# A LoRA linear layer with a retrieval feed-forward in float32 on one core: the running sums in VectorE's order, one weight combination stored where it is made, and statistics once per batch

## The reference

```
h   = x @ W.T + base_bias + (x @ A[id].T) @ B[id].T        # [8, 512, 2048]
q   = h @ Wq.T;  scores = router(q);  top 8 of 512; softmax; weighted sum of aux_values
aux = (...) @ Wvd.T @ Wvu.T
var = variance of h over the 2048 features, per token
norm_var = log1p(var) / (mean over all 4096 tokens of log1p(var) + 1e-6)
learned  = gelu(h @ Wu1.T + bu1) @ Wu2.T + bu2
u    = clip(0.5 * norm_var + 2.5 * sigmoid(learned), 0, 5)
gate = sigmoid(gate_w1 * clip((u - 0.5) / 1.5, 0, 1) + gate_bias), 0 where under 0.05
out  = x + h + gate * aux
```

## Time and profile before

| | before |
|---|---|
| median of 3 runs | 1995.03 us (1994.07 to 2000.32) |
| the profiled execution's own time | 1995.2 us |
| its span on the core | 1993.4 us |
| mean granted TensorE clock | 0.989 |
| HBM read, written | 316.32 MB, 96.47 MB |

### The profile page before, as it was taken

The page is one execution under the profiler, slowest core; times in us unless marked ns, Lnnn a source line. Parts: engine busy times, 40 slices in busy tenths (PEclk is TensorE's granted clock), DMA queues, the critical chain, the costliest instruction groups (busy, mean ns, idle before and its releaser), DMA issues.

```text
span 1993.4 us, 24866 instructions
## 1 busy us (share of the span) xinstructions
PE 1943.9 (98%) x8682; PEld 1582.2 (79%) x8682; DVE 1262.0 (63%) x1656; ACT 693.7 (35%) x1051; POOL 400.9 (20%) x283
## 2 busy tenths in 40 slices
PE   8999999999999999999999999999999999999996
PEld 6877877888888888888888877777888888888875
DVE  5775688555467836546873643677377677667666
ACT  3422433333233433324333322344233323332332
POOL 2210122120022202002210100110433323233323
PEclk9989999999999999999999999999999999999997
DMA  7656777552367745146764434757977677777774
GB/s 268 229 190 244 254 252 258 168 173 74 131 202 232 225 147 187 45 154 210 234 208 140 159 106 171 240 184 236 326 269 270 231 244 236 229 241 237 274 275 164
DMA packets 195201, 414.46 MB, mean 208 GB/s; under 512 B 26692, under 2 KB 27716, under 8 KB 194950
## 3 DMA queue, kind: packets, MB, share of 16 engines
q1 hardware_dynamic: 150150, 324.78, 50.3%
q10 hardware_dynamic: 44928, 88.10, 11.5%
HBM read 316.32 MB, written 96.47 MB: 207 GB/s over the span
## 4 chain that ended last, share of the span: by engine, by line
PE 86%; DVE 7%; issue 3%; ACT 2%; DMA 2%; ACTq 0%; SPq 0%; DVEq 0%; POOL 0%; POOLq 0%
PE bank L1659 17%; PE bank L1660 17%; PE bank L1661 17%; PE bank L1697 6%; PE bank L1698 6%; PE bank L1699 6%; PE bank L1712 1%; PE bank L1713 1%; PE bank L1599 1%; PE bank L1600 1%; PE bank L1786 1%; PE bank L1788 1%; PE bank L1787 1%; DVE sums L1261 1%; PE bank L1767 1%
## 5 line engine op out<-in xcount | busy, mean ns | idle before, releaser
L1659 PE MATMUL bank<-xop,wsp 128*128 128x512 f32 x1792 | 710.7, 397 | 14.9 <-DVE wsp L1152 8.0
L1660 PE MATMUL bank<-xop,wsp 128*128 128x512 f32 x1792 | 701.8, 392 | 0.0
L1661 PE MATMUL bank<-xop,wsp 128*128 128x512 f32 x1792 | 700.9, 391 | 0.0
L1659 PEld LDWEIGHTS bank<-xop,wsp 128*128 128x128 f32 x1792 | 338.5, 189 | 98.6 <-DVE xop L1152 8.0
L1660 PEld LDWEIGHTS bank<-xop,wsp 128*128 128x128 f32 x1792 | 338.9, 189 | 74.5 <-issue 3.8
L1661 PEld LDWEIGHTS bank<-xop,wsp 128*128 128x128 f32 x1792 | 338.2, 189 | 72.4
L1152 DVE TENSOR_TENSOR wsp<-wraw,wsp 128x1024 fp32r<-128x1024 f32 x184 | 241.2, 1311 | 122.0 <-ACT wsp L790 121.7
L790 ACT ACTIVATE wsp<-wraw 128x1024 fp32r<-128x1024 f32 x184 | 194.0, 1054 | 204.3 <-PE bank L1661 170.9
L779 POOL TENSOR_TENSOR r_h<-r_h,r_x 128x512 f32<-128x512 f32 x128 | 172.7, 1349 | 363.7 <-DMA r_h<-h_dram 363.7
L877 ACT ACTIVATE stage<-stage 128x512 f32<-128x512 f32 x128 | 80.9, 632 | 406.1 <-DVE stage L1247 405.7
L1261 DVE TENSOR_TENSOR sums<-sums,stage 128x1024 f32<-128x1024 f32 x116 | 154.5, 1332 | 92.2 <-ACT stage L877 92.2
(11 more groups left out here) (158 smaller groups left out, 1957.9 us busy)
## 6 DMA issues: line engine op xcount, KB each, us to landing
wraw<-in_w SPq DMA_DIRECT2D x131, 512.0 KB, 3.8
xraw<-in_x SPq DMA_DIRECT2D x248, 256.0 KB, 4.2
wraw<-t_dram SPq DMA_DIRECT2D x80, 512.0 KB, 3.6
h_dram<-stage ACTq DMA_DIRECT2D x128, 256.0 KB, 3.9
hraw<-h_dram SPq DMA_DIRECT2D x128, 256.0 KB, 4.0
r_x<-in_x SPq DMA_DIRECT2D x128, 256.0 KB, 4.4
r_h<-h_dram SPq DMA_DIRECT2D x128, 256.0 KB, 3.5
out<-o_st ACTq DMA_DIRECT2D x96, 256.0 KB, 3.8
```

The lines of the kernel that those rows point to most:

```text
L1659: pe.matmul(ps, wsp[:, slot, 0, f], x_hi(i), start=(k == 0), stop=False)
L1660: pe.matmul(ps, wsp[:, slot, 0, f], x_lo(i), start=False, stop=False)
L1661: last = pe.matmul(ps, wsp[:, slot, 1, f], x_hi(i), start=False, stop=(k == HT - 1))
```

## The change

It has four parts. (1) `add_sums(g-2)` moves from the front of VectorE's step to its end, ahead of `finish(g-1)`. (2) T1 is stored by ScalarE's queue from `t_res` when `make_t1` has made it (`store_t1`), and `make_t2` waits for that store; M5 of pair 0 then loads T1 from `t_dram` as the other pairs do, two steps ahead, with nothing made or stored there. (3) `T4_AT` begins at step 16 and no longer at 18. (4) The statistics are gathered in one segment for each batch: M2 and M3 share a running sum, M4 and M5 the other. The passes stand in M3 and the next M1 at o = 3, and the one in M6 is gone. The last one moves to step 5 of row 0, with the steps that use it (variances 4 to 7, log 6 to 9, its sum 7 to 10, the mean's matmul 8 to 13, the mean 9 to 14).

```diff
-        T4_AT = {18 + o: o for o in range(HT)}
+        T4_AT = {16 + o: o for o in range(HT)}
         T3_AT = {M7 * HT - 3 + o: o for o in range(HT)}
-        T1B_AT = {M5 * HT - 3 + o: o for o in range(HT)}
...
-            early = p == 0 and q in (M7, M5)
+            early = p == 0 and q == M7
...
-            return kind == "t4" or kind == "tile" and g < PAIR and tile_of(g)[1] in (M7, M5)
+            return kind == "t4" or kind == "tile" and g < PAIR and tile_of(g)[1] == M7
...
-        SEGMENT = {M2: 0, M4: 1, M5: 1, M3: 2}
-        STATS_AT = {(M6, 1): 0, (M3, 2): 1, (M1, 2): 2}
+        STATS_AT = {(M3, 3): 0, (M1, 3): -1}
+
+        def segment(p, q):
+            return 2 * p + (q in (M2, M3))
+
+        def segment_of_batch(b):
+            return b ^ 1
+
+        def stats_at(p, q, o):
+            seg = 2 * p + STATS_AT[q, o] if (q, o) in STATS_AT else -1
+            return seg if seg >= 0 else None
...
                     else:
-                        if p == 0:
+                        if q == M5:
+                            sp.wait_ge(t_moved[o], 32)
+                        elif p == 0:
                             wait_stored(sp, "t4", o)
...
-                if p == 0 and q in (M7, M5):
-                    act.dma_start(t_dram[T3 if q == M7 else T1, o], src).then_inc(t_out[W_PLACE["tile", g] % NWR], 16)
+                if p == 0 and q == M7:
+                    act.dma_start(t_dram[T3, o], src).then_inc(t_out[W_PLACE["tile", g] % NWR], 16)
+
+            def store_t1(o):
+                act.wait_ge(t_ready, t_count("t1", o))
+                act.dma_start(t_dram[T1, o], t_res[:, o, :]).then_inc(t_moved[o], 16)
...
+                if g - 1 in T1_AT:
+                    store_t1(T1_AT[g - 1])
                 if g - 1 in T4_AT:
                     store_t4(T4_AT[g - 1])
...
             def make_t2(o):
                 wait_w(dve, "t2", o)
-                dve.wait_ge(t_ready, t_count("t1", o))
+                dve.wait_ge(t_moved[o], 32)
...
-                if o == 0 and q != M5:
+                if o == 0 and q in (M2, M4):
                     wait(dve, stats_done, seg - 1)
...
-                if g > 1 and tile_of(g - 2)[1] in H_PRODUCTS:
-                    add_sums(g - 2)
                 if g + 2 < TILES:
                     split_w_lo(g + 2)
...
-                if g in T1B_AT:
-                    make_t1_again(T1B_AT[g])
...
+                if g > 1 and tile_of(g - 2)[1] in H_PRODUCTS:
+                    add_sums(g - 2)
                 if g > 0 and tile_of(g - 1)[1] in H_PRODUCTS:
                     finish(g - 1)
...
-                    if k == 2:
-                        copy_stats(3 * NPAIR - 1)
+                    if k == 6:
+                        copy_stats(NB - 1)
...
-                elif k == 1:
-                    stats_pass(3 * NPAIR - 1)
-                elif k == 8:
+                elif k == 5:
+                    stats_pass(NB - 1)
+                elif k == 13:
```

More of the change, by code:

```diff
@@ L223, in bass_adaln_ffn @@
         xr_in = [sem(f"xr_in{i}") for i in range(NXR)]
-        tb_in = [sem(f"tb_in{i}") for i in range(HT)]
+        t_moved = [sem(f"t_moved{i}") for i in range(HT)]
         a_in = sem("a_in")
@@ L386, in t_count @@
             order = [(g, 0, "t1", i) for g, i in T1_AT.items()] + [(g, 1, "t2", i) for g, i in T2_AT.items()] \
-                + [(g, 2, "t4", i) for g, i in T4_AT.items()] + [(g, 3, "t3", i) for g, i in T3_AT.items()] \
-                + [(g, 4, "t1b", i) for g, i in T1B_AT.items()]
+                + [(g, 2, "t4", i) for g, i in T4_AT.items()] + [(g, 3, "t3", i) for g, i in T3_AT.items()]
             return [e[2:4] for e in sorted(order)].index((what, o)) + 1
@@ L523, in load_w @@
                         src = w[o, :, 0:WT]
-                    elif q == M3 or (p == 0 and q == M5):
+                    elif q == M3:
                         src = w[HT + o, :, WT:2 * WT]
                     else:
-                        if p == 0:
+                        if q == M5:
+                            sp.wait_ge(t_moved[o], 32)
+                        elif p == 0:
                             wait_stored(sp, "t4", o)
@@ L569, in load_t @@
             def load_t(o):
-                sp.dma_start(t_res[:, o, :], w[o, :, 0:WT]).then_inc(tb_in[o], 16)
+                sp.dma_start(t_res[:, o, :], w[o, :, 0:WT]).then_inc(t_moved[o], 16)
             def load_x11(k):
@@ L803, in split_w_hi @@
                     if q == M1:
-                        act.wait_ge(tb_in[o], 16)
+                        act.wait_ge(t_moved[o], 16)
                     else:
@@ L811, in split_w_hi @@
                         act.wait_ge(t_ready, t_count("t3", o))
-                    if p == 0 and q == M5:
-                        act.wait_ge(t_ready, t_count("t1b", o))
                     src = w_raw("tile", g)
                 to_hi(wsp[:, g % NW, 0, :], src).then_inc(wh_ready, 1)
-                if p == 0 and q in (M7, M5):
-                    act.dma_start(t_dram[T3 if q == M7 else T1, o], src).then_inc(t_out[W_PLACE["tile", g] % NWR], 16)
+                if p == 0 and q == M7:
+                    act.dma_start(t_dram[T3, o], src).then_inc(t_out[W_PLACE["tile", g] % NWR], 16)
+            def store_t1(o):
+                act.wait_ge(t_ready, t_count("t1", o))
+                act.dma_start(t_dram[T1, o], t_res[:, o, :]).then_inc(t_moved[o], 16)
             def store_t4(o):
@@ L1092, in _ @@
                     split_wvu_hi((k - 3) // 2)
-                if c == 0 and k == 6:
+                if c == 0 and k == 9:
                     act.wait_ge(mstep, 4)
@@ L1176, in make_t3 @@
                 g = M7 * HT + o
[L1177 to L1182, removed]
                 wait_w(dve, "tile", g)
@@ L1252, in add_sums @@
                 n = h_index(p, q, o)
-                seg = 3 * p + SEGMENT[q]
+                seg = segment(p, q)
                 into = sums[:, seg % 2, :, :]
                 dve.wait_ge(sq_ready, n + 1)
-                if o == 0 and q != M5:
+                if o == 0 and q in (M2, M4):
                     wait(dve, stats_done, seg - 1)
@@ L1263, in copy_stats @@
             def copy_stats(seg):
-                p, s = seg // 3, seg % 3
                 dve.wait_ge(stats_done, seg + 1)
[L1266 to L1272, removed]
+                dve.tensor_copy(stats[:, segment_of_batch(seg), :, :], stat_ps.rearrange("p (a t) -> p a t", a=2))\
+                    .then_inc(stats_ready, 1)
             def values_lo():
@@ L1349, in _ @@
                         split_x_lo(pp, pq, k)
[L1350 to L1353, removed]
+                if stats_at(p, q, o - 1) is not None:
+                    copy_stats(stats_at(p, q, o - 1))
                 if g == LAST + M5 * HT + 1:
@@ L1437, in variances @@
             def variances():
-                dve.wait_ge(stats_ready, 3 * NPAIR)
+                dve.wait_ge(stats_ready, NB)
                 dve.tensor_scalar(mean_t[:], stats[:, :, 0, :], 1.0 / D, None, MULT).then_inc(mstep, 1)
@@ L1511, in _ @@
                 if c == 0:
-                    if k == 2:
-                        copy_stats(3 * NPAIR - 1)
+                    if k == 6:
+                        copy_stats(NB - 1)
                     if k in (3, 5):
                         split_wvu_lo((k - 3) // 2)
-                    if k == 4:
+                    if k == 7:
                         variances()
-                    if k == 7:
+                    if k == 10:
                         sum_of_logs()
-                    if k == 9:
+                    if k == 14:
                         mean_of_logs()
@@ L1606, in stats_pass @@
             def stats_pass(seg):
-                p, s = seg // 3, seg % 3
-                pe.wait_ge(sum_ready, 4 * HT * p + (HT, 3 * HT, 4 * HT)[s])
+                p = seg // 2
+                pe.wait_ge(sum_ready, 4 * HT * p + (3 * HT, 4 * HT)[seg % 2])
                 wait(pe, stats_ready, seg)
@@ L1678, in _ @@
                             router_factor()
[L1679 to L1682, removed]
+                    if k == 5 and stats_at(p, q, o) is not None:
+                        stats_pass(stats_at(p, q, o))
             lora_b(TILES - 1)
```

## The result

| | before | after |
|---|---|---|
| median of 4 runs each | 1995.62 us (1994.07 to 2000.32) | 2029.11 us (2027.63 to 2032.15) |
| span of the profiled execution | 1993.4 us | 2028.8 us |
| mean granted clock | 0.989 | 0.985 |

The ratio is 1.0163 with a 95% interval of 1.0146 to 1.0181. The kernel is slower, as forecast, but by 33.5 us (1.6%) and not by 13.7, and so beyond the range of 1988 to 2024.

A forecast was written before the change was run, and what follows sets the result against it. TensorE, busy 98%, was taken as the bound, with VectorE's step against its tile deciding. Terms 4.2 - 5.55 - 10.3 + 3X + 3.8 gave 3X - 7.85, +13.7 at X = 7.2: 2008.7 us, range 1988 to 2024.

The forecast's parts named there:

- up to the end of M7, pair 0: Pair 0's M2 to M7: late VectorE, ring order and removed pass in M6 sum to +4.2 us, between -3 and +8.
- X: Time TensorE loses per pair to late VectorE in M4 and M5: 14c + 0.2, 7.2 us with c = 0.5.
- pair 3 and the end: Last pass -4.6 us; VectorE without cover in M3 6.6 later, h tiles 0.8, M5 about 1.0: +3.8 before the removed pass.
- c: Mean cost per VectorE step of meetings with GpSimd's additions: between 0 and 1.1 us, taken as some 0.5.
- VectorE's step: Where VectorE is late, its step becomes 5.04 us plus extras, 0.95 longer than before, against TensorE's tile of 5.69.
- The 2.76 us: Time from the start of `finish` to the next `lo` of weights, a chain through ScalarE's square and `to_hi`.
- Rival 4: Stops in M5 drop TensorE's clock, some six at 1.9 us, 11 us more: 2020; chance 0.12 together with Rival 3.
- I count two such steps: Pair 0's ring: with T4 two steps earlier, two steps of some 9 us for store and load, where today four.
- if they hold up loads, up to 2 us: T1 stores in M1 and M2 were costed at nothing, or up to 2 us should they delay loads.
- Rival 1: VectorE's step fits, not slower: c under 0.17, 1987.4 us with c = 0, 1980 with M2 good too; chance 0.16.
- Rival 2: Within 0.3%: c between 0.03 and 0.31, or M2 better and M5 as forecast, 1989 to 2001 us; chance 0.22.
- Rival 3: Every GpSimd addition meets VectorE: c = 1.1, X = 15.6, +39, 2034 us; chance 0.12 together with Rival 4.

The follow-up runs named there:

- sums_back: The changed kernel with the running sums back at the front of VectorE's step, all else kept; 1982.84 us, ratio 0.9942 to the kernel before.
- t4_back: The changed kernel with T4 made from step 18 again; 2025.03 us, ratio 1.0148 to the kernel before.
- pool_short: The changed kernel with three kinds of GpSimd's additions cut to 16 of 512 columns, so operands differ from the reference's; 1993.78 us, ratio 0.9994.
- stats_only: The kernel before with the statistics part of the change alone; 1982.73 us, ratio 0.994.
- square_later: The changed kernel, sums still late, with ScalarE's square and store one step later, behind `to_hi` of the weights; 1976.85 us, ratio 0.9909.
- x_first: square_later with T4 and T3 tiles made behind the x splits in VectorE's step; 1968.49 us, ratio 0.9855.
- six kernels named above: All the kernels that store T1 where it is made and whose VectorE isn't late; M1 and M2 together take 102.7 to 105.7 us, against 101.5 before.
- sums_only: The kernel before with the running sums alone moved to the end of VectorE's step; 2066.18 us, ratio 1.0343.
- square_later_t4_back: square_later with T4 made from step 18 on; 1971.05 us, ratio 0.9879.

## Why the prediction fell short

By the two traces the span grew by 35.4 us. Pair by pair, in the prediction's own terms:

| part | predicted | measured | error |
|---|---|---|---|
| up to the end of M7, pair 0 | +4.2 | +13.8 | +9.6 |
| M5 and M3, pair 0: X - 10.3 | -3.1 | +0.9 | +4.0 |
| pair 1: X - 1.85 | +5.35 | +9.2 | +3.8 |
| pair 2: X - 1.85 | +5.35 | +6.3 | +0.9 |
| pair 3 and the end | +1.95 | +5.15 | +3.2 |

The largest single error is pair 0's head, and next to it the term c in all pairs.

**VectorE's step was right in its mechanism.** The 2.76 us, the 1.14 for an exposed sum, M5 as the place and the `combine` as the wait all came as said. Pair 0's M5 did lose its old stops: sums_back has 45.55 there, where the earlier trace rows belong to a product of 53.95.

**The term that was mis-sized is c.** The prediction took 0.5 us a step (its own product, 1.1 x 3.1 / 5.9, is 0.58, which would have made X 8.3 and the forecast 2012). From `finish` of M4's tile 0, 14 steps on, VectorE instructions that lasted longer than others of their kind cost this, and the formula with the measured c gives this X:

| | instructions, us over their kind | c | 14c + 0.2 | X measured (M5 and M3 over 45.55 and 47.39) |
|---|---|---|---|---|
| pair 0 | 12, 11.0 | 0.79 | 11.2 | 11.2 |
| pair 1 | 12, 10.8 | 0.77 | 11.0 | 11.0 |
| pair 2 | 8, 7.9 | 0.57 | 8.1 | 8.1 |

So the formula holds to 0.1 us, and only c was too small. t4_back agrees (X of 11.6, 9.4 and 11.6 for 11.6, 9.4 and 11.6). In pool_short no instruction of that stretch lasted longer than its kind, the formula gives 0.2, and 0.7 was measured, all of it in M3: the meetings are nearly all of X.

I had worked out c from the share of a step in which VectorE can be hit, as if the additions came at any time. In pairs 1 and 2 c is 0.25 and 0.26 before, and 0.24 to 0.28 in stats_only and sums_back. VectorE being late is not what raises it: in square_later, where it isn't late, c is 0.70 and 0.55 in these pairs, and those meetings cost M5 nothing. In both pairs the high c comes with the late place of the sum.

**Rival 4, the clock, is not part of X.** In pair 1 TensorE's first stop is 3.41 us long and the matmul behind it takes 0.76 us, where after a short one it takes 0.47. The granted clock is 0.86 from 624 to 636 us and 1.00 in every other stretch of that M5: the lower of the two levels for some 3.4 us, which takes TensorE 1.7 longer. But a stop of the same length ended otherwise in pairs 0 and 3, and in pair 2 the longest in M5 is 1.51:

```profile
289.75 0.47 PE L1585 MATMUL bank<-ax,b_sp 96*128 96x512 f32 x1 [3.42 <-DVE u_t L1235]
...
632.42 0.76 PE L1585 MATMUL bank<-ax,b_sp 96*128 96x512 f32 x1 [3.41 <-DVE u_t L1235]
...
645.96 0.47 PE L1585 MATMUL bank<-ax,b_sp 96*128 96x512 f32 x1 [0.34 <-DVE u_t L1235]
...
986.44 0.47 PE L1585 MATMUL bank<-ax,b_sp 96*128 96x512 f32 x1 [1.51 <-DVE u_t L1235]
...
1374.58 0.47 PE L1585 MATMUL bank<-ax,b_sp 96*128 96x512 f32 x1 [3.47 <-DVE u_t L1235]
```

In pair 0 the clock fell only behind the restart (0.86 from 288 to 300), in pair 3 not at all (1.00 from 1370 to 1382). The table above leaves nothing for the clock: VectorE sets the pace there, and I take it that a slower TensorE waits that much less. The clock did cost time outside of X, in pair 0's M2 and M7 (below).

**Pair 0's ring: the step "I count two such steps" failed.** This is VectorE's timeline, in the place of the earlier trace rows; first the row of M6's x tiles from the trace before:

```profile
115.57 2.49 DVE L1152 TENSOR_TENSOR xop<-xraw,xop 128x512 fp32r<-128x512 f32 x4
```

```profile
123.41 2.48 DVE L1166 TENSOR_TENSOR xop<-xraw,xop 128x512 fp32r<-128x512 f32 x4
...
142.03 1.23 DVE L1182 TENSOR_TENSOR t_res<-wraw,t_res 128x1024 f32<-128x1024 f32 x1 [3.78 <-DMA wraw<-in_w]
...
160.76 1.23 DVE L1187 TENSOR_TENSOR wraw<-wraw,t_res 128x1024 f32<-128x1024 f32 x1 [3.09 <-DMA wraw<-in_w]
...
171.72 1.23 DVE L1187 TENSOR_TENSOR wraw<-wraw,t_res 128x1024 f32<-128x1024 f32 x1 [6.15 <-DMA wraw<-in_w]
...
180.59 1.23 DVE L1187 TENSOR_TENSOR wraw<-wraw,t_res 128x1024 f32<-128x1024 f32 x1 [4.09 <-DMA wraw<-in_w]
182.87 2.49 DVE L1166 TENSOR_TENSOR xop<-v_t,xop 128x512 fp32r<-128x512 f32 x4
```

The wait of T2 in step 17 is there (142.03, a wait of 3.78), and TensorE stops behind it for 3.15 us where 2.4 were said. But three more trips of store and load are waited for, not two, and all three ahead of M7's x tiles: T4's sixth tile (160.76) also waits for a slot whose T4 tile is being stored. Before, two stood ahead of the x tiles and two behind. The x tiles start at 182.87, 12.2 later than in the earlier trace rows and not 4.8. TensorE's timeline at both stops:

```profile
148.01 0.76 PE L1657 MATMUL bank<-xop,wsp 128*128 128x512 f32 x1 [3.15 <-DVE wsp L1166]
...
183.61 0.79 PE L1657 MATMUL bank<-xop,wsp 128*128 128x512 f32 x1 [7.54 <-DVE xop L1166]
```

Both restart at the lower level (0.76 and 0.79 us), and from 184 to 200 us the granted clock is 0.86, where M7 before had 1.00 throughout. x_first shows the cause at M7: with the x tiles ahead of the waits the stop of 8.89 us is 0.57.

Ahead of that M6's x tiles come at 123.41, 7.8 later than the 115.57 of the kernel before and not 4.3. What failed here is less VectorE's step in M2 than the stretch in which T1 is stored, costed at nothing: TensorE itself starts M6 6.0 us later. M2 takes 5.4 us longer, and 4.6 of them lie in its first two tiles, before any of its sums is made: a stop for M2's own last x tiles, which the kernel before didn't have, and a granted clock of 0.86 from 72 to 84 us. TensorE's timeline:

```profile
71.57 0.49 PE L1657 MATMUL bank<-xop,wsp 128*128 128x512 f32 x1 [2.65 <-DVE xop L1166]
```

The prediction's "if they hold up loads, up to 2 us" names the case and is too small in this trace. That the stores hold up the loads isn't shown by itself: M1 and M2 take 1 to 4 us longer in the six kernels named above, but sums_only, without these stores, has a stop of 1.1 us at that place too.

**Statistics: right.** The terms were -5.55, -1.85 within the head and -4.6 at the last pass, 12.0 in all; stats_only gained 12 to 13.

**The end: too small.** The last pass takes 1.84 us without a wait, as said. But the stop before the first tiles of `u_pass` was to be one of about 8 us; it became three, of which the second is the larger, and M3 and M5 of pair 3 paid 2.9 and 3.2 us instead of nothing and 1.0. TensorE's timeline:

```profile
1421.38 0.50 PE L1693 MATMUL bank<-h_sp,wu 128*128 128x512 f32 x1 [0.83 <-DVE stage L1255]
...
1426.66 0.79 PE L1693 MATMUL bank<-h_sp,wu 128*128 128x512 f32 x1 [4.32 <-DVE stage L1255]
...
1429.61 0.79 PE L1693 MATMUL bank<-h_sp,wu 128*128 128x512 f32 x1 [1.31 <-DVE stage L1255]
...
1445.85 1.84 PE L1610 MATMUL bank<-ones,sums 128*128 128x1 f32 x16
```

The 6.46 us of stops take the place of the 3.04 of the earlier trace rows and of 1.17 ahead of it. The clock falls here as it did before (0.74 from 1420 to 1440 us, and 0.74 from 1385 to 1405 in the trace before; 1.00 in stats_only at that place). So what the last pass gives back is spent.

**Rivals 1 to 3.** Rival 1 needed c under 0.17; measured 0.57 to 0.79. Rival 2 fell with it. Rival 3 wanted X = 15.6; measured 11.2, 11.0 and 8.1, though its 2034 us is nearer to the result than the forecast, by the head's error and not by its own mechanism. The rule of the Trainium skill (SBUF — State Buffer, two separate sides) agrees with the rows: instructions with two SBUF inputs were stretched (the sum at 608.76 to 2.31, in square_later the split at 627.30 to 1.78), while `finish`, with a PSUM input, took at most 0.75 in all 128 cases, 16 of them beside an addition of GpSimd. A copy with one SBUF input was stretched too, 1.79 us where six of the eight take 0.68 to 0.69; for a float32 copy from SBUF to SBUF that section has the lock as well.

```profile
590.27 1.79 DVE L1266 COPY sums<-stage 128x1024 f32<-128x1024 f32 x1
```

What stays open: why the late place of the sum meets GpSimd two to three times as often as the early one, and why M1 and M2 vary by 3 us between kernels that are alike there (102.7 to 105.7).

## What to carry to other kernels

A wait on a half idle engine is a good place for work: before moving an instruction out of it, write the engine's step as a chain through the other engines and compare its length, meetings with other engines included and counted for the new order, with the tile of the engine that bounds the kernel. If the step is over, break the chain (here: square one step later) before trimming the work. An operation that may wait for a transfer goes to the back of the in-order queue, behind what needs no transfer; only then does starting it earlier pay.

## What the runs showed of the hardware that was not expected

- An engine that is 20% busy can cost another one's time. With 100 us less of GpSimd's work in pool_short (301.3 us busy for 401.8), VectorE was busy 56 us less and the kernel took 35 us less, because VectorE's step was at TensorE's limit. square_later, with its step below the limit, kept the same additions (VectorE is busy 1250.0 us in both kernels) and lost nothing to them in M5.
- TensorE came back at its lower level after stops of 3.15, 3.41, 4.32 and 7.54 us, with matmuls of 0.76 to 0.79 us, and at the higher, with 0.47 to 0.50, after stops of 1.51, 2.65, 3.42 and 3.47, and of 3.72 in square_later_t4_back. The length of a stop alone doesn't decide it.
